# A selective-scan kernel: blocks of the in-projection and the convolution between the transposes, and the convolution's copy and projection one step later

## The chip, the cores and the metric

The kernel runs on one core of a Trainium2 chip. The metric is the device time of one execution in microseconds. All data are fp32. TensorE is called PE here, VectorE DVE, ScalarE ACT, GpSimd POOL, and SyncE SP.

## What is computed

One layer on x of shape (1, 1024, 64, 64): a convolution-like stage, then a bidirectional selective scan on 4096 tokens of 1024 channels. The change touches the second part only.

```
xz = (hidden @ in_proj_w.T).transpose(0, 2, 1)          # x and z, 2048 channels each
x, z = split(xz)
# per direction (forward; backward on reversed x):
xc    = causal_depthwise_conv(x, 4 taps) + bias
x_dbl = xc @ xproj_w.T                                   # dt 64, B 16, C 16
dt    = clip(x_dbl[:64] @ dtproj_w.T + b, 1e-5, 1)
delta = softplus(dt + b);  u = clip(xc, -10, 10)
h_n   = exp(delta * A_n) * h_n(previous) + delta * u * B_n     # n = 0..15
y     = sum_n h_n * C_n + u * D
# then
out = ((y_fwd + y_bwd) * silu(z)) @ out_proj_w.T ; x + out
```

## The kernel before

**Stages.** Norms and the channel scan come first (to about 560 us), then `stage_scan` (to about 7280 us), then `stage_out`. The change lies in `stage_scan` (lines 549 to 1266).

**Units.** The scan stage works unit by unit. A unit is one block of 128 channels on one chunk of 512 tokens: 16 blocks x 8 chunks x 2 directions = 256 units (`NU`), the backward direction first (units 0 to 127), then the forward one. Every engine has its own `unit(b)` with a loop over 16 steps n, one per state, and they meet by semaphores alone. There is no planner: the order on each engine's queue is the order written by hand in its `unit`.

- DVE (lines 1217 to 1266): a scan for each n (line 1231), and for ten of the states a weighing of the scanned h by C (line 1241, `hc`). The weighings stand behind the scans in this order: scans 0, 1, 2, weighings 0, 1; scans 3, 4, 5, weighing 3; scans 6, 7, 8, weighings 6, 7; scans 9, 10, 11, weighing 9; scans 12, 13, weighings 12, 13; scans 14, 15, weighings 14, 15.
- POOL: `w` = du x B in four groups of four states (line 1179), the weighing by C of states 2, 5, 8, 11 (line 1188, `hp`), u and du of the next unit.
- ACT (lines 978 to 1143): the decay exp(delta x A_n) of each n (line 1074), the copy of the scan's last column to `state` (line 1054, which the weighing two steps back waits for), the softplus chain of the next unit (lines 983 to 1007), u x D (line 1106, `ud`), and copies out of PSUM: `in_copy` (line 1014), `xc_copy` (line 1017), `turn_copy` (line 1040), `yT_copy` (line 1033). Decays are double-buffered, so ACT runs at most two scans ahead of DVE.
- PE (lines 825 to 975): transposes that sum the ten hc, the four hp and ud into `yT` (lines 962, 923, 954; 4 records each). States 4 and 10 are turned first (`turn`, line 858, at steps 8 and 12), copied by ACT and multiplied by a diagonal of C (`add_turned`, line 867). Beside them stand the matmuls that prepare later units: the in-projection (`in_proj`, line 836, 8 matmuls of 512 columns), the convolution (line 843, 4 matmuls by diagonal matrices), `project` (line 848, 1 matmul) and the dt matmul (line 831). An fp32 matmul of 512 columns shows as two records.

**Which unit prepares what.** `inputs_of(b)` gives the input a = b + 17 whose convolution and projection unit b carries (units 0 to 238; unit 0 has two inputs, 16 and 17). `in_steps_of(b)` gives the in-projection: in the backward half that of x for the same a as long as a is itself backward (units 0 to 110), in the forward half that of z for unit b itself (units 128 to 255). So units 111 to 127 have convolution and projection without in-projection, and units 239 to 255 have an in-projection without convolution.

**The steps.** The dicts `NORMAL`, `EARLY` and `LATER` (lines 638 to 640) place this work: `into` the steps of the two halves of the in-projection, `copy` ACT's `in_copy`, `conv` the convolution, `xc` ACT's copy of it, `proj` the projection. `EARLY` and `LATER` serve unit 0 alone. Within one step PE issues in this order (lines 918 to 965): transposes of hp if n is 5, 8, 11 or 14; dt matmul; in-projection; convolution; projection; add_turned and turn; at step 11 the transposes of ud; the transposes of hc(n) if n is one of DVE's ten states. Steps 2, 4, 5, 8, 10 and 11 have no hc transposes. Queues are in order, so PE stands at hc(n) until DVE's weighing is done:

```
pe.wait_ge(S["hc_done"], b * NV + i + 3)          # line 958
```

**What hangs on PE.** DVE's scans of states 2, 4, 5, 8, 10, 11 write four `hs` buffers in turn. Scan 11 takes the buffer of state 4, so it waits for the turn of step 8 (`h_turn_mm`, line 1228); scan 5 of the next unit waits for the turn of step 12. `in_copy` waits for the last in-projection matmul (line 1012), and the decays behind it on ACT wait with it. In the backward half the convolution waits for `in_copy` (line 904). The dt matmul and the convolution share one PSUM bank, `dt_ps`, so the dt matmul of step 13 waits for `xc_copy` (line 935). In a chunk's last unit ((b + 1) % 16 == 0, called a boundary unit) the dt matmul of the next unit stands at step 0, ahead of the in-projection (line 928), and ACT's softplus chain is three steps later.

**SP** issues all DMAs in order (lines 746 to 796). In a unit it stores x behind `in_copied`, xc behind `xc_copied`, waits for all stores, then for `proj_mm`, and loads weights and inputs for input a + 2.

Of the kernel before, what the change touches and what calls it, by code (L numbers as in the profile page):

```python
# [14 lines left out]
KT = C // P  # L15
# [8 lines left out]
TAPS = 4  # L24
# [524 lines left out]
def stage_scan(nc, ident, hnT_d, winx_d, winz_d, wx_d, wdt_d, convp_d, par_d, skip_d,  # L549
               x_pad_d, xc_d, z_d, bc_d, yT_d):  # L550
    with Scope(nc, "scan") as sc:
# [3 lines left out]
        diag = sc.sb("diag", [P, 2, TAPS, P])  # L555
# [4 lines left out]
        proj = sc.sb("proj", [XO, T])  # L560
# [6 lines left out]
        xc = sc.sb("xc", [P, 2, T])  # L567
# [15 lines left out]
        dt_ps, in_ps = sc.ps("dt_ps", [P, T]), sc.ps("in_ps", [P, T])  # L583
# [6 lines left out]
        S = {n: sc.sem(n) for n in names}  # L590
# [9 lines left out]
        def back(i):  # L600

            return i % NU < HALF
# [32 lines left out]
        def decay(b, n):  # L635
            return prm[:, block_of(b), n:n + 1]

        NORMAL = dict(into=(0, 2), diag=1, copy=7, conv=5, xc=10, proj=11)
        EARLY = dict(into=(0, 2), diag=1, copy=5, conv=5, xc=8, proj=8)
        LATER = dict(into=(8, 10), diag=6, copy=11, conv=11, xc=12, proj=13)  # L640

        def inputs_of(b):

            if b == 0:
                return [(DB, EARLY), (DB + 1, LATER)]
            return [(b + DB + 1, NORMAL)] if b + DB + 1 < NU else []

        def in_steps_of(b):

            if not back(b):  # L650
                return [(b, NORMAL)]
            return [(a, when) for a, when in inputs_of(b) if back(a)]
# [3 lines left out]
        def turn_steps(b):  # L656
            if b == 0:
                return dict(mm=(6, 12), copy=(10, NS - 1), add=(12, NS - 1))
            return dict(mm=(8, 12), copy=(12, NS - 1), add=(12, NS - 1))
# [166 lines left out]
        def _(pe):  # L826

            def dt_matmul(b):
                pe.wait_ge(p_in[b % 2], (b // 2 + 1) * (NPL * LOAD))
                pe.wait_ge(S["proj_copied"], b // DB + 1)  # L830
                nc.tensor.matmul(dt_ps[:], wdt[:, b % 2], proj[0:R, :], start=True, stop=True).then_inc(S["dt_mm"], 1)

            def in_proj(s, i0, i1, bank=in_ps[:]):

                for i in range(i0, i1):
                    last = nc.tensor.matmul(bank, win[:, s, i], hn[:, i], start=(i == 0), stop=(i == KT - 1))  # L836
                if i1 == KT:
                    last.then_inc(S["in_mm"], 1)

            def convolution(s, rev, bank=dt_ps[:]):  # L840
                for i in range(TAPS):
                    at = HALO - i if rev else i
                    last = nc.tensor.matmul(bank, diag[:, s, i], x[:, s, at:at + T], start=(i == 0),  # L843
                                            stop=(i == TAPS - 1))
                last.then_inc(S["conv_mm"], 1)

            def project(a):
                nc.tensor.matmul(proj_ps[0:XO, :], wx[:, a % 2], xc_out[:, a % 2], start=(a % DB == 0),
# [2 lines left out]
            def turn(b, k):  # L851

                pe.wait_ge(S["scan_done"], b * NS + TN[k] + 1 + SCR)
                pe.wait_ge(S["in_copied"], (in_copies(b) if b or k else DB + 1) + 2)
                if b * NTN + k:
                    pe.wait_ge(S["h_turn_copied"], b * NTN + k)
                for tb in range(TB):
                    last = nc.tensor.matmul(in_ps[:, tb * P:(tb + 1) * P], h_slot(b, TN[k])[:, tb * P:(tb + 1) * P],  # L858
                                            ident[:], is_transpose=True, start=(tb == 0), stop=(tb == TB - 1))
                last.then_inc(S["h_turn_mm"], 1)  # L860

            def add_turned(b, k):

                pe.wait_ge(S["h_turn_copied"], b * NTN + k + 1)
                pe.wait_ge(S["c_diag_done"], b // DB * NTN + k + 1)
                for tb in range(TB):
                    last = nc.tensor.matmul(yT[:, tb], c_diag[:, k, tb], h_turned[:, tb * P:(tb + 1) * P],  # L867
                                            start=False, stop=False)
                last.then_inc(S["h_turned_used"], 1)
# [14 lines left out]
                    pe.wait_ge(a_in[s], (j + 1) * (NA * LOAD))  # L884
                    project(j * 2 + s)

            def in_step(i, half, b):

                if half == 0:
                    pe.wait_ge(win_in[i % 2], (i // 2 + 1) * LOAD)  # L890
                    pe.wait_ge(S["hn_loaded"], (i // DB + 1) * LOAD)
                    pe.wait_ge(S["in_copied"], i + 2)
                    if b or i > DB:
                        pe.wait_ge(S["h_turn_copied"], b * NTN if b else 1)
                    in_proj(i % 2, 0, KT // 2)
                else:
                    in_proj(i % 2, KT // 2, KT)

            def conv_step(a, b):
                pe.wait_ge(S["dt_read"], min(b + 2, NU))  # L900
                pe.wait_ge(S["xc_copied"], a + 2)
                pe.wait_ge(S["diag_done"], a * TAPS + TAPS)
                if back(a):
                    pe.wait_ge(S["in_copied"], a + 3)
                else:
                    pe.wait_ge(a_in[a % 2], (a // 2 + 1) * (NA * LOAD))
                convolution(a % 2, back(a))

            def project_step(a):
                if a % DB == 0:  # L910
                    pe.wait_ge(S["proj_copied"], a // DB)
                pe.wait_ge(S["xc_copied"], a + 3)
                pe.wait_ge(a_in[a % 2], (a // 2 + 1) * (NA * LOAD))
                project(a)

            def unit(b):
                ins = inputs_of(b)
                for n in range(NS):
                    if n in POOL_AT:
                        i = POOL_AT.index(n)  # L920
                        pe.wait_ge(S["hp_done"], b * NP + i + 1 + NP)
                        for tb in range(TB):
                            last = nc.tensor.matmul(yT[:, tb], hp[:, i, tb * P:(tb + 1) * P], ident[:],  # L923
                                                    is_transpose=True, start=False, stop=False)
                        last.then_inc(S["hp_used"], 1)
                    early = b + 2 < NU and (b + 2) % DB
                    late = b == 0 or (b + 1) % DB == 0
                    if n == 0 and late and b + 1 < NU:
                        pe.wait_ge(S["dt_read"], b + 1)
                        if b:  # L930
                            pe.wait_ge(S["xc_copied"], min(b + DB + 1, NU) + 2)
                        dt_matmul(b + 1)
                    if n == DT_AT and early:
                        pe.wait_ge(S["dt_read"], b + 2)
                        pe.wait_ge(S["xc_copied"], min(b + DB + 2, NU) + 2)
                        dt_matmul(b + 2)
                    for i, when in in_steps_of(b):
                        if n in when["into"]:
                            in_step(i, when["into"].index(n), b)
                    for a, when in ins:  # L940
                        if n == when["conv"]:
                            conv_step(a, b)
                        if n == when["proj"]:
                            project_step(a)
                    turns = turn_steps(b)
                    for k in range(NTN):
                        if n == turns["add"][k] and n > turns["mm"][k]:
                            add_turned(b, k)
                        if n == turns["mm"][k]:
                            turn(b, k)  # L950
                    if n == SKIP:
                        pe.wait_ge(S["ud_done"], b + 3)
                        for tb in range(TB):
                            nc.tensor.matmul(yT[:, tb], ud[:, tb * P:(tb + 1) * P], ident[:],
                                             is_transpose=True, start=False, stop=False)
                    if n in VN:
                        i = VN.index(n)
                        pe.wait_ge(S["hc_done"], b * NV + i + 3)
                        if i == 0:
                            pe.wait_ge(S["yT_copied"], b + 1)  # L960
                        for tb in range(TB):
                            last = nc.tensor.matmul(yT[:, tb], hc_slot(b, n)[:, tb * P:(tb + 1) * P],  # L962
                                                    ident[:], is_transpose=True, start=(i == 0 and tb == 0),
                                                    stop=(i == NV - 1 and tb == TB - 1))
                        last.then_inc(S["hc_used"], 1)
# [540 lines left out]
```

## Time and profile before

| | |
|---|---|
| median of 3 executions | 8332.51 us (8323.34 to 8334.0) |
| the profiled execution | 8327.64 us, its span 8325.9 us |
| mean granted clock of PE | 0.948 |
| start of the first unit | 775.6 us |
| busy: PE, DVE, POOL, ACT | 7232.1, 7202.0, 6737.9, 5330.5 us |
| line 836, in-projection | 3840 records, mean 593 ns |
| line 843, convolution | 1920 records, mean 612 ns |

How to read it: a timeline row merges like instructions that follow each other; a row of 8 records of line 836 is four matmuls. The records' durations overlap, so the pitch of PE's work is the distance of two starts. A number in square brackets is the idle time of the engine ahead of the row, with what ended it. The clock is given as a share of 2.4 GHz; its two levels are 2.4 and 1.2 GHz. The rows count time from the span's start.

### The profile page before, as it was taken

What the parts mean: (1) busy time and instruction counts of PE and PEld (TensorE: products, weight loads), DVE (VectorE), ACT (ScalarE), POOL (GpSimd) and SP (SyncE); (2) the same over time, 40 slices, a digit from 0 to 9 for tenths busy, and PEclk for the clock granted to TensorE, in tenths of its full rate; (3) what the DMA queues carried; (4) which work ended last, traced back from release to release, by engine and by line L of the source; (5) the groups of instructions that cost most, each with busy time, mean ns of one, the idle gap of its engine ahead of it and who ended that gap; (6) DMA issues with size and microseconds to landing.
All of it is one profiled execution on the core that took longest, in us unless ns stands there. A gap on an engine that the chain in (4) does not pass through costs nothing. (4 is left out here: it accounts for less than half of the span.)

```text
span 8325.9 us, 116063 instructions
## 1 busy us (share of the span) xinstructions
PE 7232.1 (87%) x32656; PEld 4473.8 (54%) x32656; DVE 7202.0 (87%) x7790; ACT 5330.5 (64%) x12487; POOL 6737.9 (81%) x2833
## 2 busy tenths in 40 slices
PE   7568989998999899977899899899888987779999
PEld 3243555555555555555555555555555555534444
DVE  6921999999999999999999999999999999934444
ACT  3743777777777777776777777777777776610000
POOL 0612999999999999999999999999999999921110
PEclk9789999999999999988899999999999998889999
DMA  3273232313232323221323232323232322154342
GB/s 86 76 199 135 66 117 69 117 66 117 69 117 66 117 69 117 67 98 43 105 76 127 80 129 75 128 80 127 76 128 81 124 98 82 44 199 139 134 141 75
DMA packets 540822, 843.96 MB, mean 101 GB/s; under 512 B 112576, under 2 KB 260032, under 8 KB 522816
## 3 DMA queue, kind: packets, MB, share of 16 engines
q1 hardware_dynamic: 540224, 837.03, 30.5%
q8 instruction: 248, 4.06, 0.2%
q14 instruction: 350, 2.87, 0.1%
HBM read 583.83 MB, written 253.02 MB: 101 GB/s over the span
## 5 line engine op out<-in xcount | busy, mean ns | idle before, releaser
L1179 POOL TENSOR_TENSOR scan_w<-scan_du,scan_bcast_b 128x2048 f32<-128x2048 f32 x1023 | 4633.4, 4541 | 3.6 <-DMA scan_bcast_b<-bc 3.6
L1231 DVE TENSOR_TENSOR_SCAN scan_h<-scan_da,scan_state,scan_w 128x512 f32<-128x512 f32 x2560 | 3178.7, 1280 | 36.6 <-ACT scan_da L1074 21.3
L1074 ACT ACTIVATE scan_da<-scan_delta,scan_prm 128x512 f32<-128x512 f32 x4096 | 2804.3, 685 | 0.0
L962 PE MATMUL scan_yT<-all_ident,scan_hc 128*128 128x128 f32 x10240 | 1514.7, 279 | 768.1 <-DVE scan_hc L1241 767.5
L962 PEld LDWEIGHTS scan_yT<-all_ident,scan_hc 128*128 128x128 f32 x10240 | 1184.8, 142 | 1447.9 <-DVE scan_hc L1241 1068.5
L1231 DVE TENSOR_TENSOR_SCAN scan_hs<-scan_da,scan_state,scan_w 128x512 f32<-128x512 f32 x1536 | 1906.1, 1265 | 59.4 <-PE scan_in_ps L858 41.0
L836 PE MATMUL scan_in_ps<-scan_hn,scan_win 128*128 128x512 f32 x3840 | 1730.8, 593 | 13.5 <-issue 13.5
L1241 DVE TENSOR_TENSOR scan_hc<-scan_h,scan_bcast_c 128x512 f32<-128x512 f32 x2560 | 1652.5, 678 | 38.4 <-ACT scan_state L1054 36.7
L1188 POOL TENSOR_TENSOR scan_hp<-scan_hs,scan_bcast_c 128x512 f32<-128x512 f32 x1024 | 1306.5, 1276 | 60.0 <-issue 54.1
L836 PEld LDWEIGHTS scan_in_ps<-scan_hn,scan_win 128*128 128x128 f32 x3840 | 693.1, 191 | 714.7 <-issue 714.7
L1054 ACT ACTIVATE scan_state<-scan_h 128x1 f32<-128x1 f32 x2560 | 433.4, 169 | 868.6 <-DVE scan_h L1231 861.3
L843 PE MATMUL scan_dt_ps<-scan_x,scan_diag 128*128 128x512 f32 x1920 | 899.4, 612 | 1.1 <-ACT scan_x L1014 1.1
L1390 PE MATMUL out_o_ps<-out_yg,out_wout 128*128 128x512 f32 x2048 | 892.6, 595 | 0.0
L1358 POOL TENSOR_TENSOR out_yf<-out_yf,out_yb 128x512 f32<-128x512 f32 x128 | 162.9, 1273 | 740.5 <-DMA out_z<-z 740.5
L923 PE MATMUL scan_yT<-all_ident,scan_hp 128*128 128x128 f32 x4096 | 644.2, 282 | 2.8 <-POOL scan_hp L1188 2.5
L1390 PEld LDWEIGHTS out_o_ps<-out_yg,out_wout 128*128 128x128 f32 x2048 | 386.5, 191 | 465.8 <-issue 465.8
L1368 ACT ACTIVATE out_sz<-out_z 128x512 f32<-128x512 f32 x128 | 80.7, 630 | 822.2 <-DMA out_z<-z 822.2
L867 PE MATMUL scan_yT<-scan_h_turned,scan_c_diag 128*128 128x128 f32 x4096 | 594.4, 293 | 0.0
L843 PEld LDWEIGHTS scan_dt_ps<-scan_x,scan_diag 128*128 128x128 f32 x1920 | 355.9, 196 | 383.9 <-issue 383.9
L867 PEld LDWEIGHTS scan_yT<-scan_h_turned,scan_c_diag 128*128 128x128 f32 x4096 | 560.4, 212 | 0.0
L1040 ACT ACTIVATE scan_h_turned<-scan_in_ps 128x512 f32<-128x512 f32 x512 | 300.6, 587 | 338.4 <-PE scan_in_ps L858 338.4
L923 PEld LDWEIGHTS scan_yT<-all_ident,scan_hp 128*128 128x128 f32 x4096 | 499.2, 146 | 8.2 <-POOL scan_hp L1188 6.8
(128 smaller groups left out, 6761.9 us busy)
## 6 DMA issues: line engine op xcount, KB each, us to landing
yT<-scan_y_out SPq DMA_DIRECT2D x257, 256.0 KB, 2.0
scan_win<-winx SPq DMA_DIRECT2D x128, 512.0 KB, 3.6
xc<-scan_xc_out SPq DMA_DIRECT2D x256, 256.0 KB, 2.0
scan_xc<-xc SPq DMA_DIRECT2D x256, 256.0 KB, 3.9
scan_bcast_b<-bc SPq DMA_DIRECT2D x64, 1024.0 KB, 8.3
scan_bcast_c<-bc SPq DMA_DIRECT2D x64, 1024.0 KB, 7.7
scan_win<-winz SPq DMA_DIRECT2D x128, 512.0 KB, 4.7
scan_x<-x_pad SPq DMA_DIRECT2D x128, 257.5 KB, 2.6
```

The costliest lines, as they stand in the source:

```text
L836: last = nc.tensor.matmul(bank, win[:, s, i], hn[:, i], start=(i == 0), stop=(i == KT - 1))
L843: last = nc.tensor.matmul(bank, diag[:, s, i], x[:, s, at:at + T], start=(i == 0), stop=(i == TAPS - 1))
L867: last = nc.tensor.matmul(yT[:, tb], c_diag[:, k, tb], h_turned[:, tb * P:(tb + 1) * P], start=False, stop=False)
L923: last = nc.tensor.matmul(yT[:, tb], hp[:, i, tb * P:(tb + 1) * P], ident[:], is_transpose=True, start=False, stop=False)
L962: last = nc.tensor.matmul(yT[:, tb], hc_slot(b, n)[:, tb * P:(tb + 1) * P], ident[:], is_transpose=True, start=(i == 0 and tb == 0), stop= ...
L1054: nc.scalar.activation(state_of(unit_, n_), h_slot(unit_, n_)[:, col:col + 1], ACT.Copy).then_inc(S["h_saved"], 1)
L1074: nc.scalar.activation(da[:, n % 2], delta[:, s], ACT.Exp, scale=decay(b, n)).then_inc(S["exp_done"], 1)
L1179: nc.gpsimd.tensor_tensor(w[:, g], du[:, s].unsqueeze(1).to_broadcast([P, G, T]), bcast_b[:, g * G:(g + 1) * G], ALU.mult).then_inc(S["w_d ...
L1188: nc.gpsimd.tensor_tensor(hp[:, i], h_slot(b, n), bcast_c[:, n], ALU.mult).then_inc(S["hp_done"], 1)
L1231: nc.vector.tensor_tensor_scan(flip(b, h_slot(b, n)), flip(b, da[:, n % 2]), flip(b, w[:, n // G, n % G]), state_of(b, n), ALU.mult, ALU.a ...
L1241: nc.vector.tensor_tensor(hc_slot(b, n), h_slot(b, n), bcast_c[:, n], ALU.mult).then_inc(S["hc_done"], 1)
L1390: last = nc.tensor.matmul(o_ps[:, q % 2], wout[:, q, b], yg[:, g, b], start=(b == 0), stop=(b == DB - 1))
```

## The change

`NORMAL` places the in-projection in four blocks of two matmuls, at steps 0, 1, 2 and 3 in place of two blocks of four at steps 0 and 2. `in_step` takes the number of blocks. The waits stay with the first block and the semaphore with the last. The convolution is issued as two taps at step `conv` and two at the step after it, for all three dicts, with the waits ahead of the first two and the semaphore behind the last. ACT's copy of the convolution goes from step 10 to 11 and the projection from 11 to 12 in `NORMAL`; in `EARLY` the projection goes from 8 to 9, in `LATER` the copy from 12 to 13.

```diff
--- before.py
+++ after.py
@@ -635,9 +635,9 @@
         def decay(b, n):
             return prm[:, block_of(b), n:n + 1]
 
-        NORMAL = dict(into=(0, 2), diag=1, copy=7, conv=5, xc=10, proj=11)
-        EARLY = dict(into=(0, 2), diag=1, copy=5, conv=5, xc=8, proj=8)
-        LATER = dict(into=(8, 10), diag=6, copy=11, conv=11, xc=12, proj=13)
+        NORMAL = dict(into=(0, 1, 2, 3), diag=1, copy=7, conv=5, xc=11, proj=12)
+        EARLY = dict(into=(0, 2), diag=1, copy=5, conv=5, xc=8, proj=9)
+        LATER = dict(into=(8, 10), diag=6, copy=11, conv=11, xc=13, proj=13)
 
         def inputs_of(b):
 
@@ -837,12 +837,13 @@
                 if i1 == KT:
                     last.then_inc(S["in_mm"], 1)
 
-            def convolution(s, rev, bank=dt_ps[:]):
-                for i in range(TAPS):
+            def convolution(s, rev, bank=dt_ps[:], taps=range(TAPS)):
+                for i in taps:
                     at = HALO - i if rev else i
                     last = nc.tensor.matmul(bank, diag[:, s, i], x[:, s, at:at + T], start=(i == 0),
                                             stop=(i == TAPS - 1))
-                last.then_inc(S["conv_mm"], 1)
+                if i == TAPS - 1:
+                    last.then_inc(S["conv_mm"], 1)
 
             def project(a):
                 nc.tensor.matmul(proj_ps[0:XO, :], wx[:, a % 2], xc_out[:, a % 2], start=(a % DB == 0),
@@ -884,17 +885,15 @@
                     pe.wait_ge(a_in[s], (j + 1) * (NA * LOAD))
                     project(j * 2 + s)
 
-            def in_step(i, half, b):
-
-                if half == 0:
+            def in_step(i, part, parts, b):
+
+                if part == 0:
                     pe.wait_ge(win_in[i % 2], (i // 2 + 1) * LOAD)
                     pe.wait_ge(S["hn_loaded"], (i // DB + 1) * LOAD)
                     pe.wait_ge(S["in_copied"], i + 2)
                     if b or i > DB:
                         pe.wait_ge(S["h_turn_copied"], b * NTN if b else 1)
-                    in_proj(i % 2, 0, KT // 2)
-                else:
-                    in_proj(i % 2, KT // 2, KT)
+                in_proj(i % 2, part * KT // parts, (part + 1) * KT // parts)
 
             def conv_step(a, b):
                 pe.wait_ge(S["dt_read"], min(b + 2, NU))
@@ -904,7 +903,7 @@
                     pe.wait_ge(S["in_copied"], a + 3)
                 else:
                     pe.wait_ge(a_in[a % 2], (a // 2 + 1) * (NA * LOAD))
-                convolution(a % 2, back(a))
+                convolution(a % 2, back(a), taps=range(0, TAPS // 2))
 
             def project_step(a):
                 if a % DB == 0:
@@ -936,10 +935,12 @@
                         dt_matmul(b + 2)
                     for i, when in in_steps_of(b):
                         if n in when["into"]:
-                            in_step(i, when["into"].index(n), b)
+                            in_step(i, when["into"].index(n), len(when["into"]), b)
                     for a, when in ins:
                         if n == when["conv"]:
                             conv_step(a, b)
+                        if n == when["conv"] + 1:
+                            convolution(a % 2, back(a), taps=range(TAPS // 2, TAPS))
                         if n == when["proj"]:
                             project_step(a)
                     turns = turn_steps(b)
```

## Rows read from the trace of the kernel before

**Rows 1.** the page's first part, whole span.

```profile
PE 7232.1 (87%) x32656; PEld 4473.8 (54%) x32656; DVE 7202.0 (87%) x7790; ACT 5330.5 (64%) x12487; POOL 6737.9 (81%) x2833
```

**Rows 2.** busy time by stretch: us, five engines (instructions), clock, DMA share, GB/s.

```profile
824.50:3597.50 2773.00, 2506.79 (x12330) 1610.14 (x12329) 2744.12 (x2862) 2127.07 (x5179) 2739.80 (x1112) 0.97 0.27 90
3624.20:4060.80 436.60, 315.24 (x1539) 220.18 (x1538) 401.35 (x417) 299.14 (x738) 400.03 (x163) 0.81 0.19 63
4060.80:6875.20 2814.40, 2525.39 (x12542) 1630.07 (x12540) 2791.82 (x2913) 2161.74 (x5267) 2790.36 (x1134) 0.98 0.31 103
...
1833.10:1857.90 24.80, 22.23 (x115) 14.21 (x114) 24.80 (x28) 19.37 (x48) 24.63 (x11) 1.00 0.21 67
1857.90:1883.20 25.30, 23.00 (x108) 14.57 (x107) 24.95 (x28) 18.99 (x47) 25.13 (x11) 0.93 0.20 65
```

**Rows 3.** waits of DVE in units 1 to 110: us, times, longest.

```profile
DVE scan_hc L1241 <- ACT scan_state L1054: 15.8, 45, 0.5
```

**Rows 4.** timeline of PE in one unit: start, us, work, count.

```profile
1834.44 3.60 PE L836 MATMUL scan_in_ps<-scan_hn,scan_win 128*128 128x512 f32 x8
1837.87 1.04 PE L962 MATMUL scan_yT<-all_ident,scan_hc 128*128 128x128 f32 x8
1838.75 3.60 PE L836 MATMUL scan_in_ps<-scan_hn,scan_win 128*128 128x512 f32 x8
...
1843.18 3.67 PE L843 MATMUL scan_dt_ps<-scan_x,scan_diag 128*128 128x512 f32 x8
1846.69 1.04 PE L962 MATMUL scan_yT<-all_ident,scan_hc 128*128 128x128 f32 x8
...
1848.00 0.60 PE L858 MATMUL scan_in_ps<-all_ident,scan_hs 128*128 128x128 f32 x4
1850.90 0.66 PE L962 MATMUL scan_yT<-all_ident,scan_hc 128*128 128x128 f32 x4 [2.29 <-DVE scan_hc L1241]
```

**Rows 5.** timeline of DVE in the same unit.

```profile
1833.07 2.46 DVE L1231 TENSOR_TENSOR_SCAN scan_h<-scan_da,scan_state,scan_w 128x512 f32<-128x512 f32 x2
...
1836.61 1.26 DVE L1241 TENSOR_TENSOR scan_hc<-scan_h,scan_bcast_c 128x512 f32<-128x512 f32 x2
...
1844.28 1.26 DVE L1231 TENSOR_TENSOR_SCAN scan_hs<-scan_da,scan_state,scan_w 128x512 f32<-128x512 f32 x1
...
1847.83 2.43 DVE L1231 TENSOR_TENSOR_SCAN scan_hs<-scan_da,scan_state,scan_w 128x512 f32<-128x512 f32 x2
```

**Rows 6.** timeline of ACT in the same unit.

```profile
1842.44 0.60 ACT L1014 ACTIVATE scan_x<-scan_in_ps 128x512 f32<-128x512 f32 x1
...
1843.30 0.69 ACT L1074 ACTIVATE scan_da<-scan_delta,scan_prm 128x512 f32<-128x512 f32 x1
...
1846.95 0.69 ACT L1017 ACTIVATE scan_xc_out<-scan_dt_ps,scan_convp 128x512 f32<-128x512 f32 x1
```

**Rows 7.** timelines of ACT and DVE in a chunk-boundary unit (47).

```profile
1994.29 0.60 ACT L1014 ACTIVATE scan_x<-scan_in_ps 128x512 f32<-128x512 f32 x1 [1.20 <-PE scan_in_ps L836]
...
1996.17 1.28 DVE L1231 TENSOR_TENSOR_SCAN scan_hs<-scan_da,scan_state,scan_w 128x512 f32<-128x512 f32 x1 [1.20 <-ACT scan_da L1074]
```

**Rows 8.** timelines of DVE and PE in the two units behind the pattern.

```profile
1881.90 1.36 DVE L1241 TENSOR_TENSOR scan_hc<-scan_h,scan_bcast_c 128x512 f32<-128x512 f32 x2 [0.35 <-ACT scan_state L1054]
...
1899.47 1.28 DVE L1231 TENSOR_TENSOR_SCAN scan_hs<-scan_da,scan_state,scan_w 128x512 f32<-128x512 f32 x1 [0.17 <-PE scan_in_ps L858]
...
1898.76 0.60 PE L858 MATMUL scan_in_ps<-all_ident,scan_hs 128*128 128x128 f32 x4
```

**Rows 9.** the page's DMA issues.

```profile
xc<-scan_xc_out SPq DMA_DIRECT2D x256, 256.0 KB, 2.0
```

**Rows 10.** sums over unit 1 with six boundary units, and over seven boundary units.

```profile
sum 182.05, PE 164.74 PEld 102.08 DVE 175.09 ACT 135.05 POOL 167.71; mean PE 23.53 PEld 14.58 DVE 25.01 ACT 19.29 POOL 23.96
...
sum 184.85, PE 163.22 PEld 102.01 DVE 175.37 ACT 132.70 POOL 183.31; mean PE 23.32 PEld 14.57 DVE 25.05 ACT 18.96 POOL 26.19
```

**Rows 11.** timeline of PE in unit 120.

```profile
3852.90 5.29 PE L843 MATMUL scan_dt_ps<-scan_x,scan_diag 128*128 128x512 f32 x8
```

## The prediction

> **What bounds the kernel now.** I read the page's first part, then the busy time by stretch, then the waits, then one unit engine by engine. The whole-kernel shares [rows 1] name no winner: PE, DVE and POOL all stand at 81% to 87%. The stretches do [rows 2]. In the scan with its in-projections VectorE is busy 2744.12 of 2773.00 us (units 1 to 110) and 2791.82 of 2814.40 us (units 128 to 239). POOL is nearly as full, 2739.80 and 2790.36. PE has slack in the sum, 2506.79 of 2773.00. So VectorE sets the length of a unit, and what moves the time is what VectorE waits for. The undisturbed unit that I take as the pattern starts at 1833.07 [rows 5] and has VectorE busy for all of its 24.8 us [rows 2]; at two decimals of its scans it is 24.78. The mean is longer, 2773.00 over 110 units or 25.21. In the first stretch VectorE waited 45 times for ACT's state copy, 15.8 us [rows 3]. The unit after the pattern is such a one: granted clock 0.93, length 25.3 [rows 2], 0.35 us of wait ahead of its last two weighings [rows 8]. The pattern unit shows PE's pause of 2.29 us behind the turn [rows 4], and it recurs; behind it the clock fell from the upper to the lower of its two levels in the one unit and not in the other.
>
> Now the one tight place. PE's queue from the unit's start to its first turn (line 858, step 8): first half of the in-projection at 1834.44, hc 0 and hc 1 at 1837.87, second half at 1838.75, then hc 3 and hp 0, the convolution at 1843.18, hc 6 and 7 at 1846.69, hp 1, the turn at 1848.00, ending 1848.60 [rows 4]. Scan 11 reuses the buffer that this turn reads. It is the second of the pair at 1847.83, so it starts at 1847.83 + 2.43 - 1.26 = 1849.00 [rows 5]. Where a turn came last, VectorE started 0.11 us behind its end, 1898.76 + 0.60 against 1899.47 [rows 8]. So the whole front of PE's queue has 1849.00 - 1848.60 - 0.11 = 0.29 us of slack. The 2.29 us in which PE idles come only after the turn.
>
> **The change, part by part.**
>
> 1. *In-projection in four blocks.* The 4 matmuls of a half are 8 records in 3.43 us (1834.44 to 1837.87), so a block of two matmuls takes 1.72. Blocks 2 and 3 stand at steps 2 and 3 with no transposes between, since step 2 issues none; together they are the old second half. New is the order block 0, hc 0, block 1, hc 1. Block 0 ends at 1834.44 + 1.72 = 1836.16. hc 0 is ready at 1836.61 + 0.67 = 1837.28 [rows 5] and PE starts 0.06 later. So PE now stands still for 1.18 us in which it used to compute. Then 1837.34 + 0.50 (hc 0: 0.66 as after any wait, less 0.16 of overlap with the next) + 1.72 (block 1) + 0.44 (hc 1) = 1840.00; blocks 2 and 3 to 1843.43; hc 3 and hp 0 as before 1.00 to 1844.43; convolution 3.51 to 1847.94; hc 6, 7 and hp 1 1.31, the turn 0.60: end at 1849.85. It was 1848.60, so 1.25 us late. Less the slack of 0.29 that is 0.96 us of VectorE, at scan 11.
>
> 2. *The same lateness reaches ACT sooner.* Its in-copy at step 7 started at 1842.44, 0.09 behind the in-projection's end (1838.75 + 3.60). Now that end is 1843.60 and the copy starts at 1843.70. The next decay started at 1843.30 [rows 6]; now it goes behind the copy (0.60) and takes 0.69, less some 0.05 of overlap in issue: done at 1844.94. Scan 8 started at 1844.28 [rows 5]: about 0.68 us of wait. It comes first and is contained in the 0.96, since the turn ends when it ends either way. Boundary units show that the path is real: there the dt matmul stands ahead of the in-projection, the copy waited 1.20 us for PE and scan 8 waited 1.20 us for the decay, an ln between them included [rows 7]. What is queued behind the late copy (state copy, decay, ud) moves with VectorE.
>
> 3. *Boundary units*, 13 with blocks: the dt matmul fills most of the new pause. I take 2 us for all; the ends are zero and 0.96 each, 12 us.
>
> 4. *Convolution in two.* Step 5 issues nothing behind it and step 6 nothing ahead, so the taps stay back to back: zero, but for the later input of unit 0, whose taps straddle steps 11 and 12. No instruction is added anywhere.
>
> 5. *Copy at step 11, project at 12.* ACT copied at 1846.95 [rows 6], 0.10 behind the convolution's end (1843.18 + 3.67). Now that end is 1848.10, and the decay of step 11 goes ahead of the copy, so ACT no longer stands waiting for the convolution. The gain is zero, since no wait of VectorE hung on it in the pattern. The project matmul changes places with the ud transposes, both behind the long pause and ahead of turn 1: zero. The dt matmul of step 13 waits for the copy, which is done near 1850.1, before the long pause ends at 1851.9. On SP's queue the stores of x and xc start 1.3 and some 2.5 us later; xc lands 2.0 later [rows 9], at about 1852, and ACT asks for it only after the next unit's start at 1858.8. The loads of weights and inputs queued behind project are used two units on. Zero. In unit 0 one decay no longer stands behind that copy: 1 us gained.
>
> 6. *The clock.* With the turn last, scan 11 and weighing 9 alone fill PE's pause: about 2.0 us in place of 2.29. So the clock goes on falling in some units. How many: 0.97 in the mean against 0.93 in a unit where it fell [rows 2] is 0.03/0.07 = 0.43 of the units. Such a unit is 0.54 longer than the pattern, as its turn 1, turned copy and state copy come late. The unit behind it paid too, 0.17 at scan 11 [rows 8]; the new pause of 1.18 swallows that. Bounds: no unit, or all. I take half, nearest to the 0.43: 0.27 per unit.
>
> The Trainium skill ("TensorE: Matmul & The Clock Gate", Part 4, PE-mode transpose) says that transposes do not count as activity of PE in the way that matmuls do. That speaks against the change, since the stretch from convolution to project, all transposes and pause, becomes longer. By it the clock would fall in every unit (rival C).
>
> **The sum.** Less six boundary units and unit 1, 182.05 us [rows 10], 103 ordinary units had a mean of 2590.95/103 = 25.15; less seven boundary units, 184.85 [rows 10], 105 had 2629.55/105 = 25.04. New: 24.78 + 0.96 + 0.27 = 26.01. So 103 x 0.86 = 88 and 105 x 0.97 = 102. Units 240 to 254 have the in-projection but no convolution: without its 3.51 the turn has room, but ACT's copy has not, 15 x 0.68 = 10. Boundary units 2. Units 111 to 127 have the convolution without the in-projection: they stay at the 436.60 of their stretch [rows 2], which is 27.3 each. Unit 0: -1. Sum +201 us. The profiled execution took 8327.64 (span 8325.9), 4.9 below the median and inside the spread of the three runs; so 8528. With the clock never falling, 56 less: 8472. Falling in each: 8584.
>
> **The rivals.**
>
> *B, the clock falls in the front.* The new pause at the unit's start puts low clock on the in-projection or the convolution, where VectorE pays for every lost microsecond. Units 111 to 127 show the price: at 0.81 the convolution took 5.29 [rows 11] instead of 3.67. 1.6 us in half of 208 units is 166 more, 8694; in a quarter, 8611. For: the clock reacts to pauses of 2 us. Against: this one is 1.2, with matmuls on both sides.
>
> *C, low clock in each unit at its old place*: 208 x 0.54 instead of half of it, 8584. This is what the skill's rule gives. The rows bear it out in part only: the same transposes stand in both units of rows 2, and the one kept 1.00.
>
> *D, the other side: faster.* PE being 1.25 later, its pause after the turn shrinks, the clock never falls, and the losses behind it vanish: 103 x 0.37 + 105 x 0.26 = 65 us, 8263. The place is scan 11. It decides if PE's lateness there stays under the slack of 0.29, for which hc 0 would have to be ready a microsecond before VectorE's row says.
>
> *E, no change.* The change does less than it says: blocks 2 and 3 are one, the taps are one. If the first split cost nothing too, 8328.
>
> **How the numbers follow.** Forecast, with the clock falling in about half of the units: 0.66. C 0.10, B 0.14, D 0.06, E 0.04. Slower is all but D and E: 0.90. About 0.2% (17 us) is what a measurement of this kernel can tell from no change. The likeliest case's own range is 8472 to 8584; if only ACT's 0.68 counted and no clock, it would be about 8417. For 8 in 10 I take 8440 to 8640, which leaves out D, E and the upper half of B.
>
> **What would show it.** In an ordinary unit of the changed kernel: four records of line 836, a wait of 1.2 us for hc 0, four more, then eight; VectorE waiting for ACT's decay (scan 8, 0.7 us) and for line 858 (scan 11, 0.25 us); a unit of 25.7 to 26.3 us. ACT's wait for the convolution at line 1017 is gone, and PE's busy time is unchanged. It is wrong if hc 0 is not waited for, if the turn ends less than 1 us later, or if the mean clock of units 2 to 110 leaves 0.95 to 0.99.

## The result and the profile after

The changed kernel takes 8516.77 us (median of 4 executions, 8510.77 to 8525.54) against 8333.26 us before (median of 4): a ratio of 1.0224, 95% interval 1.0208 to 1.0240. It is slower by 184 us. The forecast was 8528, with a range of 8440 to 8640.

The page's first part, with the busy time of each engine, and the busy time by stretch of units 1 to 110, 112 to 127, 128 to 239 [rows 2] and 240 to 255 (us, then PE, PEld, DVE, ACT, POOL, clock, DMA share, GB/s):

```profile
PE 7330.3 (86%) x32656; PEld 4505.2 (53%) x32656; DVE 7235.5 (85%) x7790; ACT 5279.5 (62%) x12487; POOL 6749.2 (79%) x2833
...
823.20:3690.00 2866.80, 2546.90 (x12325) 1616.84 (x12324) 2760.61 (x2862) 2106.20 (x5178) 2746.68 (x1112) 0.97 0.26 87
3717.60:4153.00 435.40, 314.15 (x1529) 219.53 (x1529) 400.22 (x416) 300.68 (x735) 398.86 (x163) 0.81 0.19 62
4153.00:7051.70 2898.70, 2575.68 (x12542) 1650.81 (x12541) 2808.06 (x2913) 2130.95 (x5267) 2797.01 (x1135) 0.96 0.30 100
7051.70:7465.00 413.30, 325.65 (x1617) 231.72 (x1616) 397.75 (x414) 274.47 (x662) 388.28 (x158) 0.88 0.17 57
```

The computing is the same; the units are longer. Units 1 to 110 went from 2773.00 to 2866.80 us, units 128 to 239 from 2814.40 to 2898.70 [rows 2]. Units 111 to 127, which have no in-projection, did not move (16 of them in 435.40 against 436.60). VectorE's idle time in the first stretch rose from 28.9 to 106.2 us, 77 of the 94. The rest shows as busy time: back to back VectorE's instructions overlap by 0.08 to 0.09 us [rows 5], and behind a wait that overlap is gone. So a wait of 0.58 in the rows makes what follows 0.66 late. The clock's mean is 0.97 as before in the first stretch, 0.96 against 0.98 in the second.

The waits of DVE by cause (us in total, times, longest), in units 1 to 110 and then in units 128 to 239:

```profile
DVE scan_hs L1232 <- ACT scan_da L1075: 68.3, 110, 1.2
DVE scan_hc L1242 <- ACT scan_state L1055: 19.7, 57, 0.5
DVE scan_hs L1232 <- PE scan_in_ps L859: 17.5, 104, 0.2
...
DVE scan_hs L1232 <- ACT scan_da L1075: 69.2, 112, 1.2
DVE scan_hc L1242 <- ACT scan_state L1055: 20.5, 59, 0.4
```

The first row is as good as new: VectorE waits in every unit for a decay of ACT, at scan 8, where before it did so 9 times in 6.0 us, and the third row was 39 times in 6.5 us. The wait for the state copy [rows 3] comes 57 times instead of 45. Now one unit with its timeline: PE in unit 41, which starts at 1864.17 (start, us, work, count, idle before):

```profile
1865.53 1.88 PE L836 MATMUL scan_in_ps<-scan_hn,scan_win 128*128 128x512 f32 x4
1868.42 0.66 PE L963 MATMUL scan_yT<-all_ident,scan_hc 128*128 128x128 f32 x4 [1.01 <-DVE scan_hc L1242]
1868.91 1.88 PE L836 MATMUL scan_in_ps<-scan_hn,scan_win 128*128 128x512 f32 x4
...
1871.07 3.60 PE L836 MATMUL scan_in_ps<-scan_hn,scan_win 128*128 128x512 f32 x8
...
1875.51 3.67 PE L843 MATMUL scan_dt_ps<-scan_x,scan_diag 128*128 128x512 f32 x8
...
1880.33 0.60 PE L859 MATMUL scan_in_ps<-all_ident,scan_hs 128*128 128x128 f32 x4
1882.95 0.68 PE L963 MATMUL scan_yT<-all_ident,scan_hc 128*128 128x128 f32 x4 [2.03 <-DVE scan_hc L1242]
```

ACT and DVE in the same unit:

```profile
1874.77 0.60 ACT L1015 ACTIVATE scan_x<-scan_in_ps 128x512 f32<-128x512 f32 x1 [1.19 <-PE scan_in_ps L836]
...
1875.31 0.69 ACT L1075 ACTIVATE scan_da<-scan_delta,scan_prm 128x512 f32<-128x512 f32 x1
...
1876.04 1.28 DVE L1232 TENSOR_TENSOR_SCAN scan_hs<-scan_da,scan_state,scan_w 128x512 f32<-128x512 f32 x1 [0.58 <-ACT scan_da L1075]
...
1881.03 1.28 DVE L1232 TENSOR_TENSOR_SCAN scan_hs<-scan_da,scan_state,scan_w 128x512 f32<-128x512 f32 x1 [0.17 <-PE scan_in_ps L859]
```

Against [rows 4]: one block of four records, then PE stands until 1868.42 for hc 0, four more, then eight. The turn ends at 1880.93, which is 16.76 us after the unit's start, where it was 15.53. ACT waits 1.19 for the in-projection, its decay of scan 8 runs at 1875.31 instead of right behind the decay before it, and scan 8 waits 0.58. At scan 11 VectorE waits another 0.17 for the turn, at 1881.03, again 0.10 behind its end.

### The profile page after: what moved, and what is told of

Same layout as the page of the kernel before. It is cut to its first block and busy times, and to the rows that moved or that the text cites. A ratio compares the mean times of both kernels' runs of the same rounds, so it can differ in the third digit from the quotient of the medians.

```text
span 8510.0 us, 116063 instructions
## 1 busy us (share of the span) xinstructions
PE 7330.3 (86%) x32656; PEld 4505.2 (53%) x32656; DVE 7235.5 (85%) x7790; ACT 5279.5 (62%) x12487; POOL 6749.2 (79%) x2833
## 5 line engine op out<-in xcount | busy, mean ns | idle before, releaser
L963 PE MATMUL scan_yT<-all_ident,scan_hc 128*128 128x128 f32 x10240 | 1575.4, 282 | 861.9 <-DVE scan_hc L1242 861.6
L836 PE MATMUL scan_in_ps<-scan_hn,scan_win 128*128 128x512 f32 x3840 | 1770.8, 594 | 12.3 <-issue 12.3
L836 PEld LDWEIGHTS scan_in_ps<-scan_hn,scan_win 128*128 128x128 f32 x3840 | 674.6, 191 | 600.0 <-issue 600.0
L868 PEld LDWEIGHTS scan_yT<-scan_h_turned,scan_c_diag 128*128 128x128 f32 x4096 | 587.1, 213 | 188.6 <-issue 188.6
```

## The experiments

All are compared with the kernel before on the same chip, whose median was 8324.75 to 8328.13 us there. "Ordinary units" are units 1 to 110 and 128 to 239 with no dt matmul at their step 0; their lengths are the distances of VectorE's scan 0 from one unit to the next.

**The in-projection in four blocks alone.**

```diff
-        NORMAL = dict(into=(0, 2), diag=1, copy=7, conv=5, xc=10, proj=11)
+        NORMAL = dict(into=(0, 1, 2, 3), diag=1, copy=7, conv=5, xc=10, proj=11)
```

> The in-projection in four blocks alone; convolution, its copy and the projection stay as before. Theory (the pause of PE at hc 0 makes the first turn late and VectorE pays at scan 11): the whole loss is here, 8333 + 184 = about 8517 us, within 10 of the changed kernel, ordinary units of 25.76 (backward) and 25.55 us (forward). Rival (the later copy and projection cost part of it, by a longer stretch without matmuls at which the clock falls): clearly less than the changed kernel, 8450 to 8500.

Measured 8518.3 us, ratio 1.0234 (1.0217 to 1.0251), 194 us above the kernel before. VectorE's wait for the decay was 68.3 us in units 1 to 110, as in the changed kernel. The whole loss is in this part.

**The rest of the change alone.**

```diff
-        NORMAL = dict(into=(0, 2), diag=1, copy=7, conv=5, xc=10, proj=11)
+        NORMAL = dict(into=(0, 2), diag=1, copy=7, conv=5, xc=11, proj=12)
```

with the taps in two and the other two dicts as in the change.

> The convolution in two, its copy and the projection one step later, the in-projection in two halves as before. Theory: no cost, 8325 to 8335 us, ordinary units of 24.78, 25.17 and 25.33 us as before, a microsecond gained in unit 0. Rival (the longer stretch without matmuls lets the clock fall in more units): the units with low clock go from about 0.4 to nearly all, 8333 + 60 = 8390 us.

Measured 8325.63 us, ratio 0.9997 (0.9987 to 1.0006). No effect. The same stretch of both kernels, before first:

```profile
900.00:3500.00 2600.00, 2350.81 (x11560) 1508.70 (x11559) 2573.53 (x2683) 1995.98 (x4860) 2573.01 (x1044) 0.97 0.27 91
...
900.00:3500.00 2600.00, 2350.90 (x11556) 1513.97 (x11555) 2572.73 (x2683) 1980.03 (x4852) 2572.96 (x1044) 0.97 0.27 91
```

The clock is 0.97 in both, though transposes alone now stand between convolution and projection for 0.4 us longer. A low clock in every unit, as in rival C, did not come of it. The Trainium skill ("TensorE: Matmul & The Clock Gate", Part 4, PE-mode transpose) says that transposes don't count as activity of PE in the same way; this run can say only that 0.4 us more of them in a row did not lower it: 0.97 in both, and low clock in 0.38 and 0.34 of the ordinary units of the two directions, against 0.38 and 0.32 before.

**The first block of three matmuls, and of one.** From the kernel before:

```diff
-        NORMAL = dict(into=(0, 2), diag=1, copy=7, conv=5, xc=10, proj=11)
+        NORMAL = dict(into=(0, 1, 2), diag=1, copy=7, conv=5, xc=10, proj=11)
...
+                cuts = (0, 3, 4, KT) if parts == 3 else (0, KT // 2, KT)
```

The blocks are of 3, 1 and 4 matmuls; with `(0, 1, 4, KT)` in the last line they are of 1, 3 and 4.

> The kernel before with the in-projection in blocks of 3, 1 and 4 matmuls at steps 0, 1 and 2. Block 0 ends 3 x 0.86 = 2.58 us after its start at 1.36, and hc 0 is ready at 4.27: pause 0.33, turn late by 0.40, of which the slack of 0.29 hides all but 0.1 (backward) and all (forward). Theory: 8333 to 8350 us, that is one quarter of the matmuls moved costs nearly nothing. Rival (splitting itself costs, or cost goes with the number of matmuls moved): half of the 184 us, about 8425.

> The kernel before with the in-projection in blocks of 1, 3 and 4 matmuls. Block 0 ends at 2.22, pause 2.05 us, everything to the turn 2.12 us late: 1.83 us of VectorE per backward unit, 1.6 per forward unit, ordinary units of about 26.6 and 26.4 us. Theory: cost is (pause less slack), some 8700 us (8670 to 8740). Rival (cost goes with the number of blocks, the same three as with 3, 1, 4): the same time as with 3, 1, 4.

Measured with three: 8334.81 us, ratio 1.0013 (1.0004 to 1.0023). Measured with one: 8753.53 us, ratio 1.0515 (1.0498 to 1.0533). Both have the same three blocks. With 3, 2 and 1 matmuls ahead of hc 0 the loss is 10, 194 and 429 us (differences of medians; for 2 that of the blocks alone). The first matmul that leaves costs almost nothing, since the slack of 0.29 us [rows 4, 5] covers nearly all of its lateness. The second adds 184 us. The third adds 235: 0.86 us in each of the 209 ordinary units (25.76 to 26.62 in the backward half, 25.56 to 26.41 in the forward one) is 180, units 240 to 254 add 19 and the boundary units 12, and the rest is the clock, which falls in 0.77 and 0.55 of the ordinary units instead of 0.53 and 0.41. That kernel is some 50 us slower than expected and outside the range. Its clock, in units 1 to 110 and 128 to 239, and its pause ahead of hc 0:

```profile
831.40:3810.00 2978.60, 2591.70 (x12326) 1640.04 (x12325) 2766.28 (x2862) 2111.64 (x5179) 2747.83 (x1112) 0.95 0.25 84
4273.40:7273.00 2999.60, 2584.18 (x12539) 1644.67 (x12538) 2808.77 (x2914) 2154.62 (x5267) 2798.93 (x1135) 0.96 0.29 96
...
888.89 0.66 PE L961 MATMUL scan_yT<-all_ident,scan_hc 128*128 128x128 f32 x4 [1.87 <-DVE scan_hc L1240]
```

0.95 and 0.96 against 0.97 and 0.98 [rows 2]. It falls more often, but hardly in more places: of 150 falls in these two stretches one lies in the front (unit 180, behind a pause of 2.07 us); all but one of the others stand at the old place behind the first turn, 18 us or more into the unit. Rival B did not come even here.

**The two paths, one at a time.** The changed kernel with ACT's in-copy one step later, so that the decay of scan 8 goes first:

```diff
-        NORMAL = dict(into=(0, 1, 2, 3), diag=1, copy=7, conv=5, xc=11, proj=12)
+        NORMAL = dict(into=(0, 1, 2, 3), diag=1, copy=8, conv=5, xc=11, proj=12)
```

> The changed kernel with ACT's in-copy at step 8 instead of 7, so the decay of scan 8 no longer stands behind it. In the changed kernel VectorE waits 0.58 us at scan 8 for the decay and 0.17 at scan 11 for the turn. Theory (the wait at scan 8 is contained in the turn's lateness): the wait at scan 8 goes and 0.75 appears at scan 11; forward units keep 25.55; backward ones 25.8 to 26.0 since the convolution waits for the copy; 8510 to 8545 us. Rival (the two waits add up, so the copy is worth its own 0.58): 208 x 0.58 less, about 8395.

Measured 8514.48 us, ratio 1.0222 (1.0208 to 1.0236): nothing gained. The waits of DVE in units 1 to 110 and 128 to 239:

```profile
DVE scan_hs L1232 <- PE scan_in_ps L859: 119.4, 110, 1.1
...
DVE scan_hs L1232 <- PE scan_in_ps L859: 73.6, 111, 0.7
```

The wait for the decay is gone from the list, and the wait for the turn has taken its place: 119.4 us in 110 waits where it was 17.5 in 104, and 73.6 in 111 where there was none. The forward half is the clean case: its undisturbed units stay at 25.56. So there the 0.58 was contained in the turn's lateness and not added to it. In the backward half the convolution waits for the copy, 0.2 us in each unit, and the undisturbed units go from 25.76 to 25.98. Units 240 to 254, which have no convolution ahead of the turn, got shorter by the move, from 390.3 to 373.7 us in all: there the decay was the path that cost, as step 2 of the prediction has it. These and fewer falls of the clock (in 0.38 and 0.46 of the ordinary units, against 0.47 and 0.51) even out.

The reverse: in the changed kernel half of the convolution leaves the front, so that the turn has room, and ACT's in-copy stays at step 7 (the copy of the convolution goes to step 12 with it).

```diff
+        NORMAL = dict(into=(0, 1, 2, 3), diag=1, copy=7, conv=5, conv2=9, xc=12, proj=12)
...
-                        if n == when["conv"] + 1:
+                        if n == when["conv2"]:
```

> The changed kernel's in-projection in four blocks, with half of the convolution moved out of the front to step 9. PE's pause of 1.0 to 1.2 us at hc 0 is still there, but the turn has slack, so only ACT's path is left: in-projection late, copy late, decay late, 0.58 us at scan 8. Theory: that wait alone, ordinary units of 25.45 instead of 25.76, in the whole 8280 + 0.5 x 208 + 10 = about 8390 us, clock up. Rival (the turn was all of it, ACT's wait is only a shadow of it): about 8285, the time without the blocks.

Measured 8406.31 us, ratio 1.0095 (1.0080 to 1.0111). VectorE's waits, in the same two groups:

```profile
DVE scan_hs L1232 <- ACT scan_da L1075: 68.4, 110, 1.2
...
DVE scan_hs L1232 <- ACT scan_da L1075: 69.3, 112, 1.2
```

Nearly nothing is left but the decay, 0.6 us per unit. Beside the same kernel without the blocks (8280, below) that is 126 us: the size of two thirds of the loss by ACT's path alone, though the two paths overlap and are not shares of a sum. Now both paths opened, `conv2=9` with `copy=8`:

> As the last one, with the in-copy at step 8: both paths by which the pause reaches VectorE are now open wide. Theory: the pause at hc 0 still stands in PE's timeline and costs nothing, ordinary units of 24.9 to 25.0, 8265 to 8295 us. Rival (four blocks cost something beside these two paths): 8330 or more.

Measured 8274.86 us, ratio 0.9935 (0.9920 to 0.9951). PE's timeline in one of its units:

```profile
1827.51 1.88 PE L836 MATMUL scan_in_ps<-scan_hn,scan_win 128*128 128x512 f32 x4
1830.40 0.66 PE L963 MATMUL scan_yT<-all_ident,scan_hc 128*128 128x128 f32 x4 [1.01 <-DVE scan_hc L1242]
1830.90 1.88 PE L836 MATMUL scan_in_ps<-scan_hn,scan_win 128*128 128x512 f32 x4
...
1840.82 0.60 PE L859 MATMUL scan_in_ps<-all_ident,scan_hs 128*128 128x128 f32 x4
```

The same four records, the same 1.01 us in which PE stands before hc 0, and no loss. It is faster than the kernel before. The pause is not what costs; its way to VectorE is. With the in-projection back in halves and nothing else changed:

> The last kernel with the in-projection back in two halves: the pause at hc 0 is gone and nothing else differs. Theory (four blocks are free once both paths are open, and POOL at 24.96 us per unit is the bound): the same within 10 us, 8265 to 8285. Rival (the blocks cost or gain something of their own): a difference of more than 15 us from 8275.

Measured 8275.55 us, ratio 0.9935 (0.9921 to 0.9949), the same within 1 us. As the units stand at some 24.96 us by then for another reason (POOL, below), a cost of the blocks under about 0.1 us per unit would not show (an estimate, from 24.96 less the 24.87 of undisturbed units below).

**The other way round: part of the convolution out of the front.** The kernel before, two taps at step 5 and two at step 9, where PE pauses for 2.3 us, with ACT's copy of the convolution and the projection at step 12:

```diff
-        NORMAL = dict(into=(0, 2), diag=1, copy=7, conv=5, xc=10, proj=11)
+        NORMAL = dict(into=(0, 2), diag=1, copy=7, conv=5, conv2=9, xc=12, proj=12)
```

> The opposite of the change, to beat both: the kernel before, with the second half of the convolution out of the tight front, in PE's pause of 2.3 us ahead of hc 9 (step 9), the copy and projection at step 12. The front gets 1.72 us shorter, so the first turn is early by some 0.5 us more (it then waits for weighing 7), and the long pause becomes two of about 1.2 and 0.6. Theory: the clock stays up in ordinary units (mean 0.99 or more in units 2 to 110), nearly all of them last 24.8; units 111 to 127 lose less at scan 11; 8333 - 65 - 25, about 8240 (8220 to 8280). Rival (the lost 0.3 us per unit is not the clock's, or the later copy makes decay 13 late): 8325 or more.

Measured 8280.44 us, ratio 0.9946 (0.9933 to 0.9960): faster than both, but 40 us slower than the 8240 of the expectation and just above its range. Three taps and one instead:

> The split of the convolution at steps 5 and 9 with three taps and one instead of two and two. PE's pauses in an ordinary unit become 0.3 us ahead of hc 6 and 1.9 us ahead of hc 9, where two and two gave 1.0 and 0.9. The last tap ends near 16.1, so ACT's copy no longer delays the decay of scan 13 (0.05 to 0.1 us of wait each). If the clock stays up over a pause of 1.9: 8270 to 8280 us, a little better than 8280. If a pause of 1.9 is enough to let it fall (it fell behind 2.0 and 2.3): mean clock of units 2 to 110 back at 0.97 to 0.98 and 8300 to 8325.

Measured 8280.23 us, ratio 0.9942 (0.9929 to 0.9956), mean clock 1.00 in units 1 to 110: no better than two and two. The question of the longer pause stays open: in unit 41 the turn waited 0.48 us for POOL's hp 1, and the pause ahead of hc 9 was 1.17 us and not 1.9.

The clock did what was expected with two and two, units 1 to 110 and 128 to 239:

```profile
825.30:3585.00 2759.70, 2498.79 (x12330) 1545.26 (x12330) 2739.82 (x2862) 2134.39 (x5179) 2735.92 (x1111) 1.00 0.28 91
...
4019.70:6830.00 2810.30, 2517.31 (x12532) 1568.50 (x12531) 2789.51 (x2913) 2171.25 (x5266) 2790.84 (x1134) 1.00 0.31 103
...
1841.65 1.25 PE L965 MATMUL scan_yT<-all_ident,scan_hc 128*128 128x128 f32 x8 [1.03 <-DVE scan_hc L1244]
...
1843.18 0.60 PE L859 MATMUL scan_in_ps<-all_ident,scan_hs 128*128 128x128 f32 x4
...
1846.38 0.66 PE L965 MATMUL scan_yT<-all_ident,scan_hc 128*128 128x128 f32 x4 [0.87 <-DVE scan_hc L1244]
```

PE's pauses are 1.03 and 0.87 where there was one of 2.29, the turn ends 0.3 us earlier, and the clock is 1.00 instead of 0.97. But most of the gain is not there. Of the 45 us between the profiled executions, units 1 to 110 give 13 and units 128 to 239 give 4; units 111 to 127, which have no in-projection, give 29 (463.4 to 434.7 us). There PE's convolution stood ahead of a turn that VectorE waited for. The waits in those units before and now, and their stretch now:

```profile
DVE scan_hs L1231 <- PE scan_in_ps L858: 29.0, 16, 1.9
...
DVE scan_hs L1234 <- PE scan_in_ps L859: 3.5, 7, 0.6
...
3585.00:4019.70 434.70, 313.68 (x1636) 217.59 (x1635) 424.22 (x444) 319.95 (x784) 427.18 (x174) 0.84 0.24 80
```

So of the 65 us that the clock was to give back 17 came. The ordinary units lie at 25.02 on average (25.16 backward and 25.04 forward before) and not at the 24.78 of the pattern. Two things hold them. The later copy on ACT makes the decay of scan 13 late: undisturbed units are 24.87, which is the expectation's second rival in small. And POOL falls behind. It is busy 2735.92 of 2759.70 us, 99.1% (VectorE 99.3%), and falls back against VectorE: its first hp starts 3.75 us into unit 2 (which starts at 851.14), 4.97 into unit 13, and 7.18 into unit 22 (which starts at 1350.45), about 0.1 more with each unit and 2.5 at the start of a chunk, where it makes two C diagonals. From unit 20 to 31 it falls back no further, and VectorE goes at POOL's pace, in units of 24.93 to 24.99. The way is seen in unit 22; the first row is POOL's in unit 2:

```profile
854.89 1.28 POOL L1191 TENSOR_TENSOR scan_hp<-scan_hs,scan_bcast_c 128x512 f32<-128x512 f32 x1
...
1357.63 1.31 POOL L1191 TENSOR_TENSOR scan_hp<-scan_hs,scan_bcast_c 128x512 f32<-128x512 f32 x1
...
1363.36 1.29 POOL L1191 TENSOR_TENSOR scan_hp<-scan_hs,scan_bcast_c 128x512 f32<-128x512 f32 x1
...
1364.71 0.66 PE L924 MATMUL scan_yT<-all_ident,scan_hp 128*128 128x128 f32 x4
...
1367.62 0.69 ACT L1020 ACTIVATE scan_xc_out<-scan_dt_ps,scan_convp 128x512 f32<-128x512 f32 x1 [0.35 <-PE scan_dt_ps L843]
...
1368.13 2.66 DVE L1234 TENSOR_TENSOR_SCAN scan_h<-scan_da,scan_state,scan_w 128x512 f32<-128x512 f32 x2
```

POOL's hp 1 ends at 1364.65, PE turns it right then, the second half of the convolution comes behind it, ACT waits 0.35 for that, and scans 12 and 13 take 2.66 instead of 2.46. With three taps and one the copy's part is gone (23 units of 24.79), and POOL's lateness comes by hp 1 and the turn to scan 11 instead: the same 8280.

Single units of the kernel with both paths open (units 2, 58 and 49), and what PE waited for from 2025 to 2055:

```profile
850.29:875.20 24.91, 22.48 (x114) 14.02 (x113) 24.91 (x28) 19.25 (x49) 24.74 (x11) 1.00 0.26 80
...
2252.76:2277.74 24.98, 22.55 (x114) 14.01 (x113) 24.91 (x28) 19.26 (x49) 24.81 (x11) 1.00 0.19 68
...
2025.62:2053.02 27.40, 25.11 (x120) 16.43 (x121) 25.00 (x27) 19.24 (x49) 27.23 (x12) 0.94 0.19 61
...
PE scan_yT L922 <- POOL scan_hp L1189: 2.3, 2, 2.1
```

Most units are 24.91 to 24.98 long. In 11 of the 14 chunks the second unit takes 27.3 to 28.0: just before it POOL makes the two C diagonals of the chunk, 2.5 us that it has no slack left to hide, and PE waits for its hp. So of the 90 us counted (65 for the clock, 25 for units 111 to 127) 47 to 53 came. That POOL is the bound of the long units is read from these rows; no run took work from it.

## Why the prediction was right

**The place and the mechanism** are as forecast. All of the loss comes with the four blocks (step 1): block 0 ends early, PE stands before hc 0, the first turn ends 1.23 us late (forecast 1.25), and scan 11 starts at 16.86 against 15.93 us into the unit, 0.93 late (forecast 0.96). The ordinary backward unit with full clock is 25.76 (forecast 25.74). The pause in the profile is 1.01, not 1.18, because the last record of a block is longer than the pitch by which I reckoned; hc 0 starts at the reckoned time.

**ACT's path** (step 2) came at scan 8, which starts 11.87 us into the unit instead of 11.21: 0.66 late, forecast 0.68 (0.58 of it is idle time in the row). It was contained in the turn's lateness, as the copy at step 8 shows. In the forward half it weighs more than the prediction said, since the turn is not last there. A forward unit that starts at 5006.34, PE and DVE:

```profile
5017.12 0.60 PE L922 MATMUL scan_yT<-all_ident,scan_hp 128*128 128x128 f32 x4
5017.56 3.60 PE L843 MATMUL scan_dt_ps<-scan_x,scan_diag 128*128 128x512 f32 x8
...
5022.30 0.60 PE L859 MATMUL scan_in_ps<-all_ident,scan_hs 128*128 128x128 f32 x4
...
5018.22 1.28 DVE L1232 TENSOR_TENSOR_SCAN scan_hs<-scan_da,scan_state,scan_w 128x512 f32<-128x512 f32 x1 [0.58 <-ACT scan_da L1075]
...
5021.79 2.50 DVE L1232 TENSOR_TENSOR_SCAN scan_hs<-scan_da,scan_state,scan_w 128x512 f32<-128x512 f32 x2
```

The convolution starts 0.44 behind hp 0, not 0.56, as it does not wait for the in-copy there, and takes 0.08 less. The turn ends at 5022.90. Scan 11 is the second of the pair at 5021.79, at 5021.79 + 2.50 - 1.28 = 5023.01, 0.11 behind it again, but with nearly nothing to wait for: scan 8's 0.66 has moved it to within 0.08 of there. The forward unit lasts 25.55, not 25.74. **This is the term that was mis-sized**: 105 x 0.97 = 102 us, measured 2898.70 - 2814.40 = 84. I had taken the slack of a backward unit for both halves.

**The clock** (step 6). It fell in 0.47 of the backward and 0.51 of the forward ordinary units (before 0.38 and 0.32, counted from the changes of the granted clock in the trace). Forecast was one half. The units with it last 26.29 instead of 25.76, a price of 0.53 (forecast 0.54). That the share came so near to one half owes something to luck, since the half was taken as the value nearest to 0.43 and no row fixed it: with the blocks alone it was 0.53 and 0.41. The unit behind pays nothing now: PE's 0.65 of lateness goes into the pause before hc 0.

**The sum** against the profiled executions: +94 (forecast 88 and 2 for the boundary units), +84 (102), units 240 to 254 +10 (10), unit 0 -1 (-1), units 111 to 127 zero (zero), and 3 us less outside these; 8511.8 - 8327.64 = 184 in all against 201. So the forecast of 8528 was 11 us above the median, mostly by the forward half.

**Zero as forecast**: the taps in two, the copy and the projection one step later, the transfers. ACT's wait for the convolution is gone from the profile, and it bought nothing, since the copy was no one's last wait.

**The rivals.** The faster one (no wait at the turn, clock up) and the one of no change failed at scan 11, by the 0.29 of slack. Low clock in every unit failed too: it fell in about half, and the rest of the change alone left it at 0.97. Low clock in the front was not seen: all but one of the 115 falls in units 1 to 110 and 128 to 239 of the changed kernel lie 18 to 22 us into the unit, behind the first turn.

## What to carry to other kernels

On an in-order queue work that stands ahead of a wait is free only if it fills the time up to that wait. Cutting a block and putting the cut part behind the wait leaves a pause where work was, and everything behind it is late by that pause: find who waits at the end of that stretch, and how much slack it has, before cutting. Here the same pause cost 184 us, 126 us or nothing, by which of the two consumers had slack; and moving work from ahead of the tight wait to a pause behind it gained 47 to 53 us, half of what was counted, and most of it where the turn had been waited for; elsewhere the next engine (POOL, 99% busy) was the bound.

## What the runs showed of the hardware that was not expected

The clock fell to its lower level behind pauses of PE of 2.0 to 2.3 us with only transposes around them, in 0.3 to 0.8 of such units, and in nearly none (0.01, mean clock 1.00) once two 512-column fp32 matmuls stood in the middle and the pauses were 0.9 and 1.0 us. A pause at hc 0, with 512-column matmuls ahead of it and close behind it, did not do the same: none of 1.0 us in the changed kernel lowered the clock, and in the kernel with one matmul ahead of hc 0 none of the pauses of 1.2 to 1.9 us did, only one of 2.07. Taking the low clock away gained 17 us in units 1 to 110 and 128 to 239, where 65 were counted: at POOL's pace a unit takes some 24.96 us, where VectorE with its waits took 25.16 and 25.04.
